# Second expert product of two expert layers as three rounded passes with transposed output

## What is computed

```python
gates = jax.nn.softmax(x @ Wg + bg, axis=-1)
_, top_idx = jax.lax.top_k(gates, 2)
mask = jax.nn.one_hot(top_idx, E).sum(axis=-2)
g = gates * mask
g = g / jnp.maximum(jnp.sum(jnp.abs(g), axis=-1, keepdims=True), EPS)
h = jnp.einsum('btd,edh->bteh', x, W1) + b1      # D = 128, H = 512, E = 8
h = jax.nn.gelu(h, approximate=False)
eo = jnp.einsum('bteh,ehd->bted', h, W2) + b2
x = x + jnp.einsum('bte,bted->btd', g, eo)       # on the normalised x
```

## Time and profile before

| stretch, us from the start | what runs there |
|---|---|
| 0 to 505 | cross attention of layer 0 |
| 573.6 to 644.8 | experts of layer 0, 71.2 us |
| 644.8 to about 1430 | cross attention of layer 1 |
| 1774.6 to 1899.0 | experts of layer 2, 124.4 us |

### The profile page before, as it was taken

One profiled execution on the slowest core, in us unless ns is written; L12 is line 12 of the kernel. 1 busy time (PEld: TensorE's weight loads), 2 busy tenths in 40 slices (PEclk: granted clock), 3 DMA queues, 4 the chain that ended last, 5 costly groups with the idle time before them and its releaser, 6 DMA issues. The chain is left out here.

```text
span 2795.6 us, 44841 instructions
## 1 busy us (share of the span) xinstructions
PE 2617.1 (94%) x16865; PEld 2195.2 (79%) x16865; DVE 1780.7 (64%) x3733; ACT 1627.8 (58%) x2865; POOL 1402.9 (50%) x1111
## 2 busy tenths in 40 slices
PE   5999999898999999999988888997999999999878
PEld 4899998686999999999987766785677777777647
DVE  7888885455555555555544545527888888888572
ACT  4888886335766666666643344434666666666433
POOL 1877875111766666666720062204666756566240
PEclk9999999999999999999999999999999999999999
DMA  3333231022011111101004041202000000000000
...
DMA packets 222577, 117.88 MB, mean 42 GB/s; under 512 B 21368, under 2 KB 217633, under 8 KB 222369
## 3 DMA queue, kind: packets, MB, share of 16 engines
...
## 5 line engine op out<-in xcount | busy, mean ns | idle before, releaser
L873 POOL TENSOR_TENSOR L_xattn_held<-L_xattn_held,L_xattn_shift 128x512 f32<-128x512 f32 (+1 forms) x613 | 762.8, 1290 | 285.1 <-ACT L_xattn_shift L794 285.0
L590 PEld LDWEIGHTS L_xattn_acc<-L_xattn_rows,L_xattn_held 128*128 128x128 f32 (+2 forms) x5120 | 621.0, 192 | 34.4 <-DVE L_xattn_mixed L976 8.8
L590 PE MATMUL L_xattn_acc<-L_xattn_rows,L_xattn_held 128*128 128x129 f32 (+2 forms) x5120 | 630.4, 276 | 5.2 <-DVE L_xattn_mixed L976 5.2
L997 DVE TENSOR_TENSOR L_xattn_running<-L_xattn_ring,L_xattn_running 128x512 f32<-128x512 f32 (+1 forms) x384 | 264.2, 688 | 269.1 <-PE L_xattn_ring L572 257.3
L784 ACT ACTIVATE L_xattn_held<-L_xattn_held 128x512 f32<-128x512 f32 (+2 forms) x640 | 400.4, 631 | 0.2
L1642 POOL TENSOR_TENSOR L_xattn_projected<-L_xattn_along,L_xattn_crossed 128x512 f32<-128x512 f32 (+1 forms) x256 | 271.5, 1071 | 256.1 <-DVE L_xattn_crossed L1709 254.0
L777 ACT COPY L_xattn_held<-L_xattn_ring 128x512 f32<-128x512 f32 (+1 forms) x416 | 243.3, 585 | 227.7 <-DVE L_xattn_running L997 193.2
L570 PE MATMUL L_xattn_ring<-L_xattn_queries_hi,L_xattn_keys_hi 128*128 128x512 f32 (+2 forms) x640 | 281.3, 440 | 3.4 <-DVE L_xattn_keys_lo L901 2.0
L572 PE MATMUL L_xattn_ring<-L_xattn_queries_hi,L_xattn_keys_lo 128*128 128x512 f32 (+2 forms) x640 | 253.6, 396 | 0.0
L571 PE MATMUL L_xattn_ring<-L_xattn_queries_lo,L_xattn_keys_hi 128*128 128x512 f32 (+2 forms) x640 | 253.0, 395 | 0.0
L1346 PE MATMUL L_xattn_sums<-L_xattn_probT,L_xattn_rows 128*128 128x256 f32 (+2 forms) x896 | 242.8, 382 | 0.6 <-ACT L_xattn_mixed L1531 0.6
...
## 6 DMA issues: line engine op xcount, KB each, us to landing
...
```

The costliest lines, as they stand in the source:

```text
L590: mm = nc.tensor.matmul(acc[:, c // 2, c % 2 * WIDE:(c % 2 + 1) * WIDE], held[0:n, u % 2, k, c * P:(c + 1) * P], rows[0:n, b % 2, k, :], s ...
L873: nc.gpsimd.tensor_tensor(tile, tile, shift[0:keys_of_tile[k]], ALU.subtract).then_inc(shifted, 1)
L997: seen = nc.vector.tensor_tensor(most, bank, most, ALU.max)
```

## The change

`moe_wide_stage` takes the place of `moe_stage` in layers 0 and 2. The first product is as before. New are:

- ACT runs the activation twice per chunk: into `h_hi` (float32r) and into `hidden` (float32, two buffers). `h_ready` comes after the second.
- `h_lo = hidden - h_hi` is made on POOL for expert 0 (`first_split`) and on DVE for the others (`h_split`). ACT may write `hidden[j % 2]` again only after that subtraction.
- POOL splits `w2` as well as `w1`, into two buffers each, and now waits for the use of the buffers.
- The second product has `w2_hi` or `w2_lo` as weights and 512 moving columns of `h_hi` or `h_lo`: three passes for each half and chunk. `mix` holds output features on partitions and tokens along the row.
- The gate of a token now varies along the row, equal on all partitions. `gateT` is stored to DRAM, and each expert's row is loaded onto 128 partitions (`gate_wide`, two buffers, 512 KB a load). `mix_in(0)` waits for the first.
- At the end `acc` is turned back with eight PE transposes before it is added to `lat`.
- In `column_attention_stage`, `peak_wide` and its copy go; PE reads the peak as 128 equal columns.

Core of the diff, from the new function, with the column attention's edit first:

```diff
-                            turn = nc.tensor.transpose(turned_bank[:, c * P:(c + 1) * P], peak_wide[:, c, :], core.ident[:])
+                            turn = nc.tensor.transpose(turned_bank[:, c * P:(c + 1) * P], peak[:, c:c + 1].to_broadcast([P, P]), core.ident[:])
...
-                nc.vector.tensor_reduce(peak[:], turned_bank[:].rearrange("p (c k) -> p c k", k=P), AX, ALU.max)
-                dve.drain()
-                nc.vector.tensor_copy(peak_wide[:], over_last(peak[:], P)).then_inc(peak_ready, 1)
+                nc.vector.tensor_reduce(peak[:], turned_bank[:].rearrange("p (c k) -> p c k", k=P), AX, ALU.max).then_inc(peak_ready, 1)
...
+            sp.wait_ge(gateT_ready, 1)
+            sp.dma_start(gates_there, gateT[:]).then_inc(gate_stored, 16)
+            sp.wait_ge(gate_stored, 16)
+            for e in range(E):
+                if e >= 2:
+                    sp.wait_ge(mix_used, e - 1)
+                sp.dma_start(gate_wide[:, e % 2, :], gates_there[e].partition_broadcast(P)).then_inc(wide_loaded[e % 2], 16)
...
+                for c in range(C):
+                    if e == 0:
+                        pe.wait_ge(first_split, c + 1)
+                    else:
+                        pe.wait_ge(h_split, C * (e - 1) + c + 1)
+                    for half in range(2):
+                        part = slice(half * BANK, (half + 1) * BANK)
+                        out, hi, lo = mix[:, part], h_hi[:, e % 2, c, part], h_lo[:, e % 2, c, part]
+                        nc.tensor.matmul(out, w2_hi[:, e % 2, c, :], hi, start=(c == 0), stop=False)
+                        nc.tensor.matmul(out, w2_hi[:, e % 2, c, :], lo, start=False, stop=False)
+                        last = nc.tensor.matmul(out, w2_lo[:, e % 2, c, :], hi, start=False, stop=(c == C - 1))
+                last.then_inc(mix_done, 1)
...
+            for t in range(TILES):
+                if t % 4 == 0:
+                    pe.wait_ge(acc_ready, t // 4 + 1)
+                turn = nc.tensor.transpose(aux[t // 4][:, (t % 4) * P:(t % 4 + 1) * P], acc[:, t * P:(t + 1) * P], core.ident[:])
...
+            split_w1(0)
+            split_w2(0)
+            split_w1(1)
+            for c in range(C):
+                pool.wait_ge(h_ready, c + 1)
+                nc.gpsimd.tensor_tensor(h_lo[:, 0, c, :], hidden[:, c % 2, :], h_hi[:, 0, c, :], ALU.subtract).then_inc(first_split, 1)
+            split_w2(1)
+            for e in range(2, E):
+                split_w1(e)
+                split_w2(e)
...
+                    if j >= 2:
+                        if j - 2 < C:
+                            act.wait_ge(first_split, j - 1)
+                        else:
+                            act.wait_ge(h_split, j - 1 - C)
+                    nc.scalar.activation(h_hi[:, e % 2, c, :], hid[j % 2][:], func, bias=b1_sb[:, e, c:c + 1])
+                    nc.scalar.activation(hidden[:, j % 2, :], hid[j % 2][:], func, bias=b1_sb[:, e, c:c + 1]).then_inc(h_ready, 1)
...
+            for e in range(E):
+                if e + 1 < E:
+                    split_hidden(e + 1)
+                mix_in(e)
+            dve.wait_ge(mix_done, E + 1)
```

227 lines of the change are left out of this document (224 added, 3 removed).

## The result

The changed kernel took 2825.43 us in the median of four runs (2814.58 to 2827.0), the kernel before 2806.11 us beside it (2803.92 to 2808.92). The ratio is 1.006, with a 95% interval of 1.0033 to 1.0087: slower by 0.6%, some 17 us (9 to 24). The two medians lie 19.3 us apart. The forecast was 2827 us, with a range of 2809 to 2840. The profiled execution took 2814.58 us (span 2812.7), against 2797.42 before.

What follows compares the result with a forecast made beforehand. PE was taken to bound both expert stages and the attention loop. Layer 0 +7.3, layer 2 +10.2, clock +3.3, tails +1 and attention -1 gave +20.8 us, a median of 2827 us, range 2809 to 2840.

Steps and rivals of the forecast that it cites:

- attention edit: Attention stages: 48 copies leave DVE, but PE stands still only 4.1 of 770 us; -1 us, bounds -5 and +5.
- entry of layer 2: Layer 2's start: POOL's splits and low parts, ACT's wait and the gates' trip make expert 1's weighting 11.7 us late.
- layer 0, up to w7, with its clock: Layer 0 to the last expert's weighting: late entry less loop and product gains, +7.3 us, plus 2.3 for low clock.
- layer 2, up to w7, with its clock: Layer 2 to the last expert's weighting: 11.7 late, last product saves 1.5, so +10.2 us, plus 1.0 for low clock.
- tails of both stages: After the last weighting: addition, bias product and new turning in halves, +0.5 us each, between -0.5 and +2; +1 together.
- The trip: Gates stored to DRAM and loaded back at both entries: 2.8 us store, 0.5 issue, 4.0 load; bounds 5.5 and 9.5.
- The loop of layer 0: Layer 0's experts: 6.1 us each, between 5.6 and 7.5, with DVE and POOL meeting; a gain of 0.27 an expert.
- The clock: PE at half clock after waits of some 6 us: 2.3 us in layer 0, 1.0 in layer 2; +3.3 together.
- the lesser entry: Rival, entries: trip takes 5.5 us and clock never falls, +14, near 2820, or 2816 without DVE and POOL meeting; chance 0.13.
- a clock that stays low: Rival, layer 2: PE's pauses within each expert keep the clock low beyond the entry, 2837 us or more; chance 0.10.
- The attention did not pay back: Rival, attention: most of some 22 us of DVE copies lies on PE's path, so 2806 us, no change; chance 0.06.
- faster-than-before rival: Rival, entries: first low parts on POOL and the trip are absorbed, only loops count, -5 to -6, 2800 us; chance 0.09.

Runs made afterwards that it cites:

- e1: The kernel before with only the attention edit (no peak_wide copy, PE turns the peak as one repeated column): 2802.64 us, ratio 1.0001.
- e8: Changed kernel with gates turned before expert 0's product and expert 0's gates spread by PE instead of through DRAM: 2825.57 us, ratio 1.0099 to the kernel before.
- e11: Changed kernel with PE filler matmuls in layer 0, 24 before the product of expert 1, 10 before the last product: 2817.27 us, ratio 1.0052 to the kernel before.
- e9: Changed kernel with both layers mended (low parts, turn of the gates; layer 2 also bank release, deeper hidden): 2797.48 us against 2801.23 before, ratio 0.9984.
- e10: Mended expert stage in layer 2 alone, old stage in layer 0: 2790.33 us, ratio 0.9958 to the kernel before.

## Why the prediction was right, and where its terms were off

The verdict and the time held (2825.4 for 2827), and the mechanisms were those named: PE idle 5.4 us before the product of expert 1 behind a weighting that waits for the DMA of `gate_wide`; ACT waiting for POOL's `h_lo` in layer 2 (5.39 us before the third chunk and 0.18 before the fourth, not at four chunks; before the next it waited for PE); the weightings 12.7 us apart there; no effect of the attention edit that could be told. The lines of ACT and POOL that answer to the forecast for the entry of layer 2:

```profile
1804.17 1.11 ACT L2769 ACTIVATE L_ffn_h_hi<-L_ffn_hid,L_ffn_b 128x1024 fp32r<-128x1024 f32 x1 [5.39 <-POOL L_ffn_h_lo L2741]
...
1806.47 1.11 ACT L2769 ACTIVATE L_ffn_h_hi<-L_ffn_hid,L_ffn_b 128x1024 fp32r<-128x1024 f32 x1 [0.18 <-POOL L_ffn_h_lo L2741]
...
1797.78 0.61 POOL L2732 CAST L_ffn_w_hi<-L_ffn_w 128x512 fp32r<-128x512 f32 x1 [11.67 <-DMA L_ffn_w<-in_L_ffn_W]
...
1801.74 9.34 POOL L2741 TENSOR_TENSOR L_ffn_h_lo<-L_ffn_hidden,L_ffn_h_hi 128x1024 fp32r<-128x1024 f32 x4
```

By the terms, in the profiled executions:

| term | predicted | measured |
|---|---|---|
| layer 0, up to w7, with its clock | +7.3 + 2.3 = +9.6 | +5.1 |
| layer 2, up to w7, with its clock | +10.2 + 1.0 = +11.2 | +7.1 |
| tails of both stages | +1 | +1.2 + 1.9 = +3.1 |
| attention edit | -1 | 0 (e1, some 4 us either way) |
| all other parts | 0 | +1.8 |
| span | +20.8 | +17.1 |

- **The trip** was the term most over-priced. It was put at 7.3 us for a store of 2.8, 0.5 and a load of 4.0, from the earlier trace rows. It took 5.8 (the gates were in SBUF at 598.44, the weighting began at 604.21): the load was issued 1.8 us behind the store, and the weighting began 3.9 us later. The Trainium skill, page "DMA: Bandwidth & Descriptors", section "Anatomy of one DMA — SWDGE (gpsimd) path", had given 5.3 as an estimate, which lies nearer than the rows of 512 KB did, although its fit is for transfers that GpSimd issues, and SP issues these. The prediction put that estimate's effect at 3.5 us over both layers; 7.3 - 5.3, twice, is 4.0. Over two layers the trip is 3 us of the error.
- **The loop of layer 0** was put at 6.1 us an expert for POOL and DVE in each other's way. It ran at 5.54 (5.55 in the steps from expert 2 to 6), PE's own pace. The lock was seen (two of DVE's gate instructions took 1.91 and 1.97 us instead of 0.23 beside POOL), but in the loop DVE had room for it: it worked 21.3 of the 24 us from 612 to 636, and PE all 24. The way from w1 to w7 gained 3.9 us over the old stage (37.1 to 33.2). The prediction had 2.9 for it (1.4 + 0.8 + 0.7), with a slip: its sum starts from the product of expert 1, which is itself 0.7 us shorter, and counts the 0.7 only once. The rule of the Trainium skill on the port pair (page "SBUF — State Buffer", section "SBUF: two separate sides"), weighed in the prediction as some 3 us of the sum, fits the trace and was worth nothing in layer 0: the gates were late and still ready 1.3 us before PE came to the turn. It became worth something when the turn came sooner (e8, a wait of 1.8 us for the gates).
- **Layer 2's entry**: at w1 10.2 us late; 11.7 and 1.0 for the clock had been put down. Counted from the stage's start, the trip is 1.5 of the 2.5 us. The turned gates were in SBUF 0.9 us before the time put down without the clock: POOL began its low parts 0.7 sooner and took 9.34 us for 9.8. From weighting 0 to 1 it took 8.0 us for 7.1, since DVE's low parts of expert 2 stand ahead of weighting 1 and waited 1.1 and 0.8 us for ACT. In layer 0 w1 was put at 11.8 late with the clock, and came 9.0 late.
- **The clock** was put at 2.3 us in layer 0 and cost 1.5 to 1.9 by e11. This was the best of the terms, and the one with the thinnest rows. In layer 2 it fell where it had been put, behind PE's wait of 4.99 us for ACT (granted clock 0.50 over 1806 to 1810, passes 0.43 apart), but no run prices it there. Where it was missed is the end of the stage.
- **The tails** were under-priced, +3.1 for +1. The turn in halves puts PE, DVE, PE and DVE in line. The eight turns took 1.97 us in both tails of the changed kernel, where the eight turns of the gates took 1.03: the granted clock was 0.50 over 648 to 650 and 0.52 over 1910 to 1912.
- The sum came near since errors of both signs met: 8.6 us too much before w7; 2.1 too little in the tails, 1.8 in the parts that nothing had been put down for (below what such parts differ by from one profile to the next), and 1 in the attention. The reading of the profile was good for the sign and the places; the agreement within 2 us is partly luck.

The rivals: the lesser entry named the right misses (a trip of 5.5, DVE and POOL out of each other's way) but not the clock. The rival of a clock that stays low did not come: it was at 1.00 in layer 2 from 1814 to 1908. The attention did not pay back (e1). The faster-than-before rival said that the entry must be absorbed and POOL's part be halved; e9 and e10 absorb the entry, by edits that put the turn and the low parts elsewhere, and take ACT's hold of the bank away besides, which that rival did not ask for. They came to 2797 and 2790 us beside 2801.
